# Transposes of the identity ahead of TensorE's waits in an attention and Mamba block

## The reference

```python
x = x + xattn(layernorm(x), ctx, ctx, mask, wq, wk, wv, wo)   # 32 query heads, 8 key/value heads of 128
x = x + mamba2(layernorm(x), in_proj_w, conv_w, ...)          # 128 heads of 64, 8 groups of state 128, 16 chunks of 512 columns
x = x + ffn(layernorm(x), weight_quantized, scales, zeros, bias)

# mamba2, its end
xg = scan_out * silu(gate)
xr = xg * rsqrt(mean(xg * xg) + EPS)                          # the mean over a group of 1024 columns
return (xr * norm_weight) @ out_proj_w.T
```

## Time and profile before

| | before |
|---|---|
| median of 3 runs | 738.63 us |
| the three runs | 735.67, 738.63, 745.71 us |
| profiled execution | 734.99 us |
| its span, first to last instruction | 733.1 us |
| mean granted TensorE clock | 0.995 |
| TensorE busy | 698.3 us, 95% |
| VectorE busy | 551.2 us, 75% |
| ScalarE busy | 396.2 us, 54% |
| GpSimd busy | 300.6 us, 41% |
| data moved | 93.74 MB, mean 128 GB/s |

### The profile page before, as it was taken

One profiled execution on the slowest core, in us unless ns is written; L12 is line 12 of the kernel. 1 busy time (PEld: TensorE's weight loads), 2 busy tenths in 40 slices (PEclk: granted clock), 3 DMA queues, 4 the chain that ended last, 5 costly groups with the idle time before them and its releaser, 6 DMA issues.

```text
span 733.1 us, 11917 instructions
## 1 busy us (share of the span) xinstructions
PE 698.3 (95%) x3929; PEld 594.0 (81%) x3929; DVE 551.2 (75%) x1174; ACT 396.2 (54%) x602; POOL 300.6 (41%) x150
## 2 busy tenths in 40 slices
PE   5899999999999999999999999797979999999996
PEld 4678888888888888888888888686969998999985
DVE  5977658648848857765864874757999889998994
ACT  4364535536446446454553644653776666766752
POOL 3342404404503413230440440200268887888780
PEclk9999999999999999999999999999999999999999
DMA  9601021012001202202101200840897788787700
GB/s 321 244 26 72 1 72 57 14 47 80 16 12 59 72 0 72 72 0 72 57 14 56 72 0 0 316 175 4 311 329 305 285 321 317 294 330 303 276 25 15
DMA packets 20292, 93.74 MB, mean 128 GB/s; under 512 B 2609, under 2 KB 3761, under 8 KB 11441
## 3 DMA queue, kind: packets, MB, share of 16 engines
q1 hardware_dynamic: 20272, 93.50, 34.8%
HBM read 93.17 MB, written 0.33 MB: 128 GB/s over the span
## 4 chain that ended last, share of the span: by engine, by line
PE 87%; DVE 5%; DMA 4%; ACT 2%; issue 1%; SPq 0%; POOL 0%; POOLq 0%; DVEq 0%
PE bank L376 21%; PE bank L378 20%; PE bank L377 20%; PE bank L573 10%; PE bank L486 8%; PE bank L650 3%; PE bank L456 2%; DMA ctx_raw<-in_ctx_t 2%; DMA w_hs_sb<-in_w_hs 1%; DMA wqo_raw<-in_wo 1%; ACT probs L769 1%; PE bank L657 1%; PE bank L624 1%; PE bank L423 1%; DVE decay L1238 1%
## 5 line engine op out<-in xcount | busy, mean ns | idle before, releaser
L1395 POOL TENSOR_TENSOR wqo_lo<-wqo_raw,wqo_hi 128x2048 fp32r<-128x2048 f32 x15 | 69.5, 4632 | 207.1 <-ACT wqo_hi L705 175.6
L1070 DVE TENSOR_TENSOR pt_lo<-bank,pt_hi 128x512 fp32r<-128x512 f32 x128 | 87.7, 690 | 62.2 <-ACT pt_hi L779 62.2
L779 ACT ACTIVATE pt_hi<-bank 128x512 fp32r<-128x512 f32 x128 | 75.7, 598 | 66.0 <-PE bank L486 65.7
L1382 POOL TENSOR_TENSOR k_lo<-rope_a,k_hi 128x512 fp32r<-128x512 f32 x32 | 43.4, 1355 | 105.9 <-ACT k_hi L723 105.9
L1031 DVE CUSTOM_DVE_ANT_0 probs<-bank,mask_sb 128x512 f32<-128x512 f32 x128 | 82.2, 686 | 0.1
L486 PEld LDWEIGHTS bank<-ident,probs 128*128 128x128 f32 x512 | 63.6, 141 | 21.5 <-ACT probs L769 3.7
L486 PE MATMUL bank<-ident,probs 128*128 128x128 f32 x512 | 76.1, 274 | 4.6 <-ACT probs L760 3.3
L1425 POOL TENSOR_TENSOR w_out_lo<-w_out_sb,w_out_hi 128x2048 fp32r<-128x2048 f32 x16 | 73.4, 4587 | 17.2 <-ACT w_out_hi L880 17.2
L1430 POOL TENSOR_TENSOR w_gate_lo<-w_gate_sb,w_gate_hi 128x2048 fp32r<-128x2048 f32 x15 | 69.0, 4597 | 19.2 <-ACT w_gate_hi L872 19.2
L769 ACT ACTIVATE probs<-probs,neg_max 128x2048 f32<-128x2048 f32 x31 | 62.0, 2005 | 1.0 <-DVE neg_max L1021 0.6
L573 PE MATMUL bank<-xnT,w_hs_sb 128*128 128x128 f32 x512 | 59.7, 275 | 0.6 <-DMA w_hs_sb<-in_w_hs 0.6
(11 more groups left out here) (186 smaller groups left out, 1709.4 us busy)
## 6 DMA issues: line engine op xcount, KB each, us to landing
w_hs_sb<-in_w_hs SPq DMA_DIRECT2D x16, 1024.0 KB, 4.8
w_gate_sb<-in_w_gate SPq DMA_DIRECT2D x16, 1024.0 KB, 4.8
w_out_sb<-in_w_out SPq DMA_DIRECT2D x16, 1024.0 KB, 6.4
wqo_raw<-in_wq SPq DMA_DIRECT2D x8, 1024.0 KB, 4.8
wqo_raw<-in_wo SPq DMA_DIRECT2D x8, 1024.0 KB, 4.8
decay<-decay_rows SPq DMA_DIRECT2D x16, 512.0 KB, 6.8
ctx_raw<-in_ctx_t SPq DMA_DIRECT2D x3, 1024.0 KB, 11.0
wk_raw<-in_wk SPq DMA_DIRECT2D x8, 256.0 KB, 2.7
```

What stands on the lines that cost most here:

```text
L779: act.activation(pt_hi[t % 3], ring_b[(t + 1) % 2][:, :], ACT.Copy).then_inc(s["pt_hi_ready"], 1)
L1070: dve.tensor_tensor(pt_lo[t % 3], ring_b[(t + 1) % 2][:, :], pt_hi[t % 3].bitcast(F32), ALU.subtract)\
L1395: pool.tensor_tensor(wqo_lo[:, :, :], wqo_raw[:, :, :], wqo_hi[:, :, :].bitcast(F32), ALU.subtract)\
```

## The change

A helper `turn_identity(count, spare)` is added. It issues `count` transposes of `ident` into the first 128 columns of a PSUM bank. Nothing reads the result, and no semaphore is raised. It is called at eight places: 32 times ahead of the wait in `transpose_norm(1)` and 14 behind its transposes, 28 ahead of the last `attend`, 13 behind it, 26 ahead of the wait in `transpose_norm(2)` and 6 behind its transposes, 13 ahead of the wait for x_ready in chunk 1, and 12 ahead of the wait for y_gated in chunk 0 and in chunk 15. That makes 156 transposes. No other engine's program is changed, and no instruction is taken out.

```diff
+            def turn_identity(count, spare):
+
+                for _ in range(count):
+                    pe.transpose(spare[:, 0:P], ident[:, :], ident[:, :])
+
             def transpose_norm(n):
+                if n < 3:
+                    turn_identity((32, 26)[n - 1], bank[4])
                 pe.wait_ge(s["xn_ready"], n)
...
             transpose_norm(1)
+            turn_identity(14, bank[4])
...
             scores(G - 1)
+            turn_identity(28, bank[4])
             attend(G - 1, True)
+            turn_identity(13, bank[4])
...
             transpose_norm(2)
+            turn_identity(6, bank[4])
...
                 if first:
                     transpose_hs(n, i)
                     hs_step(1, 0)
+                elif isinstance(n, int) and n == 0:
+                    turn_identity(13, bank[6])
                 pe.wait_ge(s["x_ready"], c + 1)
...
                 if not first:
                     out_step(n + i - 1, 1 - i)
+                if first or last_chunk:
+                    turn_identity(12, bank[1] if last_chunk else bank[3])
                 pe.wait_ge(s["y_gated"], c + 1)
```

## The result

The changed kernel takes **735.08 us** (median of 22 executions, 730.76 to 738.66), the kernel before **738.25 us** (22 executions, 735.06 to 747.07). The ratio is 0.9947 with a 95% interval of 0.9923 to 0.9971: faster by 0.5%.

What follows compares the result with a forecast made beforehand. TensorE was taken as the bound, 87% of the chain that ended last. The profiled 734.99 us less 1.34, less 1.4, plus 0 gave 732.2, raised 1.8 towards the runs' median to 734.0 us; range 730.5 to 740.

Steps and rivals of the forecast that it cites:

- The two savings: Slow-clock stretches return to full clock: 1.34 us in the last attention, 1.62 us in the projections from w_gate_sb.
- Rival 1: Transposes don't keep the clock up, both 0.50 stretches stay, savings nil: 735.0 us; chance 0.27.
- VectorE as the next bound: Up to the x_skip sum VectorE can come forward only 1.3 to 1.4 us; 1.4 of the 1.62 taken.
- All transposes fit their waits: The 110 behind the start, 0.109 us each, end within their waits, such as 28 in 3.3 us; cost 0.
- The start at nothing: The 32 + 14 transposes at the start delay nothing, with 3.1 us of slack: 0, upper bound 0.5 us.
- The sum: Whole kernel: profiled execution 734.99 us less 1.34, less 1.4, plus 0, giving 732.2 us.
- Rival 2: Second saving swallowed: w_hs_sb lands no earlier with DMA queues busy, only 1.34 won, 733.7 us; chance 0.13.
- Rival 3: Transposes take 0.272 us each and outlast their waits behind the start by 16.7 us: 749.0 us; chance 0.04.

Runs made afterwards that it cites:

- start_only: Changed kernel with only the 32 + 14 transposes at the start, the other 110 left out: 737.29 us, ratio to the kernel before 0.9965.
- no_start: Changed kernel without the 32 + 14 transposes at the start, the other 110 kept: 732.36 us, ratio to the kernel before 0.9906.
- out_early: Changed kernel with the w_out_sb slot 0 load issued ahead of SyncE's wait for the stored decay rows: 732.35 us, ratio to the kernel before 0.9912.
- plain_products: Changed kernel with fp32 products of the identity, half as many, in place of the transposes: 732.64 us, ratio to the kernel before 0.9942.
- cover_two: Changed kernel plus 34 transposes ahead of the first head's q rotation and 12 ahead of the third w_hs_sb load: 731.88 us, ratio 0.9902.
- nostart_cover: Changed kernel without the start's 46 transposes, plus 28 ahead of the q rotation and 12 ahead of the third w_hs_sb load: 733.69 us, ratio 0.9926.
- before_again: The kernel before, unedited, profiled a second time: 741.51 us, mean granted clock 0.988.
- cover_out: cover_two with out_early's edit, 8 for 12 transposes ahead of the load and 18 for 28 ahead of the last attention: 731.23 us, ratio 0.9897.
- best: cover_out without the start's 46 transposes and with 20 for 34 ahead of the q rotation: 732.19 us, ratio to the kernel before 0.9899.

## Why the prediction was right, and where it wasn't

**The two savings.** Right in place and size. 1.34 and 1.62 us were read off the same work at either clock; after shows 28.47 us where before had 29.79 (1.32), and 7.26 where it had 8.88 (1.62). Rival 1 is refuted: transposes do raise and keep the clock. The plainest proof is at the start, where the identity's transposes alone went from 0.21 to 0.11 us each; and start_only, without the other 110, has both falls again, while none of the eleven profiles that have them (one with products) falls near 476 or 506. The rule that I weighed against the change, in the Trainium skill, TensorE: Matmul & The Clock Gate, section "Part 4: PE-mode transpose", says that the full rate doesn't engage for transposes; it differs from these rows, and the rows decide.

**VectorE as the next bound.** I gave 1.4 of the 1.62. From xn's transposes to the x_skip sum before took 36.84 us, no_start 35.01, out_early 35.02, plain_products 35.26, cover_two 35.70: 1.1 to 1.8 us less. VectorE's convolution pauses went (in after its 48 steps on bc_acc run without one), so the step held, and 1.4 lies inside what came. But it comes only where w_hs_sb lands in time: nostart_cover, with a store of 3.3 us, took 36.65 and kept 0.2.

**All transposes fit their waits: wrong for 28.** The step took the wait's length, 3.3 us, from one execution. It starts at TensorE's own pace and ends at a load's. In after the exponentials that follow the load of wo came only 0.2 to 0.5 us later than before, the last needed one at 474.60, while TensorE was 1.8 us later at the end of its scores. That left 2.0 us from 472.56 on, not 3.3, and the 28 outlasted it by 1.0. So they passed on 1.0 us of the start's lateness that this wait would have taken up. The other counts fit: 13 ahead of the output projection left 0.17 us, 12 and 13 left 0.2 and 0.4, 26 ended with xn.

**The start at nothing: wrong.** The sum argued that with 3.1 us of slack nobody would notice TensorE's start. That held for the consumers: VectorE took the q projection at 20.64. It missed that TensorE, done sooner, waits longer behind K and q (3.8 to 3.95 us in five of the seven profiles that have the start's transposes and no cover, 2.2 to 3.5 in the three with neither), and that a fall behind this wait runs into a stretch that TensorE bounds. Between the two first profiles themselves little of this is TensorE's: the last matmul of K starts 0.1 us earlier in after (19.61 against 19.71), and the rotation comes 0.3 us later (23.85 against 23.55). From there to head 0's first probability transposes after takes 49.36 us and before 48.02, so the fall cost 1.34 us, and TensorE is 1.64 us late (73.21 against 71.57). The text had seen that falls come behind waits, and applied it only to the two waits that had one in this profile.

**Rival 2, with 0.13, came true in after's profile, and by more than it said.** Not the volume of loads swallowed the saving but one wait in SyncE's queue, for a store of 64 KB that takes 2.3 to 4.9 us in fourteen profiles; the kernel before has it as well (before_again, with a wait of 2.8 us). And the wait of 2.9 us was followed by a fall of 6.8, which rival 2 didn't price. In no_start, cover_two and out_early neither happened.

**Rival 3** (0.27 us a transpose) is refuted: 28 in 3.05 us, 52 in 5.67, 0.109 each.

**The sum and the median.** 734.99 less 2.7 was made against an execution with 0.995 of the clock, where the kernel's own mean is 0.987. The median fell by 3.2 us. That the two numbers are close owes something to errors that cancel: more falls were avoided than the profile showed (the tail's at 722.8 among them), and 1.0 us of outlasting and the start's new fall were paid. By the runs, the change as it might have been (cover_out) is worth 8.9 us by the medians and 7.6 by the ratio, about three times the 2.7 of the sum; its 1.0 us at the last attention, the moved load and the covered q rotation are in that.

**What the change leaves out.** From the x_skip sum of chunk 0 to the end eleven of the fourteen profiles take 192.2 us, within 0.1. The other three are before_again (194.6), best and nostart_cover (193.9 each), and these have a fall after 722 while TensorE works. In best and nostart_cover it comes in the last projection, ahead of which TensorE waits 1.1 us for the third xn and 0.7 us for xnT, and every kernel of the study leaves these two waits empty. Filling them wasn't tried; where such a fall comes it costs 1.7 to 2.4 us.

## What to carry to other kernels

Work put into a wait to keep the clock up should end before the wait does in the shortest case, not in the one profiled; where the wait's end is a load's, its length changes with all that comes before. Look at every wait behind which TensorE bounds, also those that the profile shows without a fall, and at those that the change itself makes longer. And take the mean granted clock of many executions before subtracting two profiles, and compare stages in all profiles at hand, since a single pair can mislead.

## What the runs showed of the hardware

- 128x128 f32 transposes of the identity alone raised the granted clock: in after they started at 2.04 us, 0.21 apart, and went 0.11 apart from between 6.2 and 6.4 us. In other profiles of the study with the same start the rise came between 5.9 and 8.1 us, with products between 5.0 and 5.3.
- Stretches at 0.50 cost, by the distance between the same instructions: 1.3 us behind the q rotation (3.4 us long), 1.34 in the last attention, 1.62 in the projections from w_gate_sb, 1.7 and 2.4 at the end (3.4 and 6.8 us long).
- A store of 64 KB took 2.4 us in one profile and 4.8 in another of nearly the same program, and the two w_out_sb loads behind it in SyncE's queue were issued 5.6 us after it and not 3.3.
- Executions of one program differed by 8 us (after) and 12 us (before); with nearly every wait filled (cover_out) the spread was 2.2 us, 730.4 to 732.59, in six.
